# Ranking's row sums moved from VectorE to ScalarE over four row buffers, and the projection's bias moved from GpSimd to VectorE

## The reference, cut to what matters

```python
score = einsum('bc,bnc->bn', gt, kproj) * SCALE         # per batch, after a layer norm of x
probs = softmax(score, axis=-1)
order = argsort(-probs, axis=-1)                        # 3136 tokens ranked
reserve = order[:, :1568]
...                                                     # merging, attention with top-k, back to tokens
out = (full + x_prune) @ W_proj + b_proj                # then x + out, layer norm, routing to 8 experts
```

## Time and profile before

| what | us |
|---|---|
| median of 3 runs | 11960.32 (11940.51 to 11967.36) |
| the profiled execution | 11958.84 |
| its span | 11957.0 |
| `rank` with the constants, about 0 to 1411 | 1411 |
| `merge`, about 1411 to 3010 | 1599 |
| `attend`, about 3010 to 10368 | 7358 |
| `project`, about 10368 to 11089 | 721 |
| `experts`, about 11089 to 11957 | 868 |

### The profile page before, as it was taken

One profiled execution on the slowest core, in us unless ns is written; L12 is line 12 of the kernel. 1 busy time (PEld: TensorE's weight loads), 2 busy tenths in 40 slices (PEclk: granted clock), 3 DMA queues, 4 the chain that ended last, 5 costly groups with the idle time before them and its releaser, 6 DMA issues. The chain is left out here.

```text
span 11957.0 us, 167569 instructions
## 1 busy us (share of the span) xinstructions
PE 8171.2 (68%) x45521; PEld 5352.0 (45%) x45521; DVE 9191.7 (77%) x26006; ACT 6947.3 (58%) x11527; POOL 2151.1 (18%) x1960
## 2 busy tenths in 40 slices
PE   5555477777486765667878687876667768343899
PEld 4555455555243433334444344443334434233787
DVE  8999644444898988999999899998889989644333
ACT  0000011221697976878999799997788979122222
POOL 2323211111000000000000000000000000277666
PEclk9999955555566655656666666665666656555555
DMA  3222100000000000000000000000000000243211
GB/s 91 73 68 72 33 19 20 20 19 21 14 16 16 17 12 14 13 16 17 17 17 18 14 15 18 18 18 14 13 14 17 18 12 16 43 96 79 55 54 40
DMA packets 669893, 352.03 MB, mean 29 GB/s; under 512 B 587281, under 2 KB 605680, under 8 KB 665056
## 3 DMA queue, kind: packets, MB, share of 16 engines
q1 hardware_dynamic: 607920, 242.84, 9.5%
q0 software_dynamic: 58624, 60.72, 2.0%
q10 hardware_dynamic: 2384, 37.11, 0.9%
HBM read 200.20 MB, written 147.72 MB: 29 GB/s over the span
## 5 line engine op out<-in xcount | busy, mean ns | idle before, releaser
L1049 PE MATMUL a_psT<-a_qt,a_kt 74*122 74x366 bf16 x3456 | 1554.8, 450 | 969.1 <-ACT a_pT L1130 632.0
L1138 ACT ACTIVATE a_junk<-a_s,a_aim 122x1097 bf16<-122x1097 f32 x1152 | 1378.9, 1208 | 721.3 <-DVE a_s L1281 721.3
L1214 DVE MAX8 a_near<-a_below 122x8 f32<-122x274 f32 (+1 forms) x4608 | 1699.2, 430 | 0.1
L1052 PEld LDWEIGHTS a_psT<-a_weigh,a_drops 122*122 122x122 bf16 x10368 | 1571.0, 190 | 192.0
L1207 DVE SCALAR_TENSOR_TENSOR a_below<-a_s,a_te,a_signs 122x1097 f32<-122x1097 f32 x1152 | 1546.4, 1352 | 129.2 <-remote 128.3
L1130 ACT ACTIVATE a_pT<-a_psT 122x732 f32<-122x732 f32 (+1 forms) x1920 | 1371.6, 715 | 455.4 <-PE a_psT L1052 447.9
L1052 PE MATMUL a_psT<-a_weigh,a_drops 122*122 122x122 bf16 x10368 | 1522.5, 273 | 0.0
L1138 ACT ACTIVATE a_signs<-a_s,a_te 122x1097 bf16<-122x1097 f32 x1152 | 1400.9, 1219 | 4.4 <-DVE a_te L1199 4.4
L1065 PE MATMUL a_psO<-a_pT,a_v 122*32 122x366 f32 x6912 | 1401.3, 698 | 0.0
L1138 ACT ACTIVATE a_junk<-a_s,a_te 122x1097 bf16<-122x1097 f32 x1152 | 1389.2, 1209 | 0.0
L1049 PEld LDWEIGHTS a_psT<-a_qt,a_kt 74*122 74x122 bf16 x3456 | 616.8, 178 | 1667.0 <-issue 1648.1
(11 more groups left out here) (356 smaller groups left out, 14795.9 us busy)
## 6 DMA issues: line engine op xcount, KB each, us to landing
xbuf<-r_blank ACTq DMA_DIRECT2D x16, 1990.6 KB
e_xg<-xbuf SPq DMA_DIRECT2D x56, 568.8 KB, 4.3
r_bc<-pr SPq DMA_DIRECT2D x16, 1372.0 KB, 7.4
a_k<-kT SPq DMA_DIRECT2D x384, 51.5 KB
a_q<-qT SPq DMA_DIRECT2D x384, 51.5 KB
a_kt<-kT SPq DMA_DIRECT2D x384, 51.5 KB
a_qt<-qT SPq DMA_DIRECT2D x384, 51.5 KB
r_xt<-in_x SPq DMA_DIRECT2D x16, 784.0 KB
```

Of the source, the lines that this page charges most:

```text
L1049: pe.matmul(out[:, x, 0:CW], kt[q][:, u * QP:(u + 1) * QP], qt[q][:, c * CW:(c + 1) * CW], start=True, stop=False)
L1052: mm = pe.matmul(out[:, x, t * QP:(t + 1) * QP], drops[:, c * CT + t, u * QP:(u + 1) * QP], weigh[:, :], start=False, stop=t == CT - 1)
L1138: act.activation(out[:, :], s_[:, t, :], ACT.Sign, bias=at[:, t:t + 1], scale=-1.0, accum_out=total[:, t:t + 1]).then_inc(counted[r], 1)
L1214: mx = dve.max(near[:, t, g, :], below[t % 3][:, EDGES[g]:EDGES[g + 1]])
```

## The change

In `rank` the comparison no longer adds up its rows (except for the last tile). ScalarE reads the marks of tile j and copies them to a scratch buffer with an accumulating output, which gives the row sums. VectorE waits for this count (`row_counted`) beside TensorE's before it writes over a mark buffer, and once more at a batch's end. ScalarE's square and root for the next batch come behind its copies 1 and 6. The parts are placed behind other comparisons. The rows `xls` and the indices get four buffers instead of two, and the body of a batch is written out twelve times (four, a loop that turns twice over four, four).

In `project` the bias is added by VectorE: batches 0 and 1 ahead of everything, batch b + 2 behind `seat(b)`. GpSimd issues no tensor instruction there any more. `merge` clears 17 semaphores of the ranking before its first load.

```diff
-BEHIND = [0, 1, 8, 10, 11, 12, 13, 14, 15, 16]
+BEHIND = [0, 5, 10, 12, 13, 14, 15, 16, 17, 18]
+LAPS = 4
...
-        xls = [sb(f"r_xl{u}", [TP, NT, C + 1]) for u in range(2)]
+        xls = [sb(f"r_xl{u}", [TP, NT, C + 1]) for u in range(LAPS)]
...
+        spill = [sb(f"r_spill{i}", [TP, N], BF16) for i in range(2)]
...
+            for u in range(LAPS):
+                body(0, u, True, True)
+            if B > 2 * LAPS:
+                with eng.Fori(1, B // LAPS - 1) as i:
+                    for u in range(LAPS):
                         body(i, u, False, True)
+            for u in range(LAPS):
+                body(B // LAPS - 1, u, False, u < LAPS - 1)
...
         @block.scalar
-            with act.Fori(0, B) as b:
+            def body(i, u, first, more):
+                b = LAPS * i + u
                 act.dma_start(d.xbuf[...], blank[...]).then_inc(cleared, 16)
+                for j in range(NT - 1):
+                    act.wait_ge(compared, (NT - 1) * b + j + 1)
+                    if j >= 2 or not first or u:
+                        act.wait_ge(row_counted, (NT - 1) * b + j - 1)
+                    act.activation(spill[(u + j) % 2][:, j * TP:N], greater[j % MARKS][:, j * TP:N], ACT.Copy,
+                                   accum_out=cnt[:, 1, j:j + 1]).then_inc(row_counted, 1)
+                    if more and j == BEHIND[0] + 1:
+                        square(b + 1)
+                    if more and j == BEHIND[1] + 1:
+                        deviate(b + 1)
...
         @block.vector
                     if j >= MARKS:
                         dve.wait_ge(added, (NT - 1) * b + j - MARKS + 1)
-                    more_ = dve.tensor_scalar(greater[j % MARKS][:, at:N], bc[:, at:N], rk[:, j:j + 1], None, ALU.is_gt,
-                                              ALU.add, accum_out=cnt[:, 1, j:j + 1])
+                        dve.wait_ge(row_counted, (NT - 1) * b + j - MARKS + 1)
                     if j < NT - 1:
-                        more_.then_inc(compared, 1)
+                        dve.tensor_scalar(greater[j % MARKS][:, at:N], bc[:, at:N], rk[:, j:j + 1], None,
+                                          ALU.is_gt).then_inc(compared, 1)
...
-                            dve.wait_ge(scattered[1 - u], 16 * NT * (i + u))
+                        v = (u + 1) % LAPS
+                            dve.wait_ge(scattered[v], 16 * NT * (i if v else i + 1))
...
+                dve.wait_ge(row_counted, (NT - 1) * (b + 1))
...
 merge, sync:
+            for used in k.used:
+                sp.sem_clear(used)
             rows(0)
...
 project, gpsimd:
-            def bias(b):
-                pool.wait_ge(x_in[u], 16 * (b // 2 + 1))
-                pool.tensor_tensor(xts[u][:, :, :], xts[u][:, :, :], bproj[...].to_broadcast([TP, NT, C]),
-                                   ALU.add).then_inc(biased, 1)
-            bias(0)
-            bias(1)
             place(pool, k, d, B - 1, 0, srcs, dsts, src_in, dst_in, put)
             for b in range(B):
-                if b + 2 < B:
-                    bias(b + 2)
 project, vector:
+            def bias(b):
+                dve.wait_ge(x_in[b % 2], 16 * (b // 2 + 1))
+                dve.tensor_tensor(xt[:, :, :], xt[:, :, :], bproj[...].to_broadcast([TP, NT, C]),
+                                  ALU.add).then_inc(biased, 1)
+            bias(0)
+            bias(1)
             normalise(0)
             for b in range(B):
                 if b + 1 < B:
                     normalise(b + 1)
                 choose(b)
                 seat(b)
+                if b + 2 < B:
+                    bias(b + 2)
```

More of the change, by code:

```diff
@@ L219, in rank @@
         rks = [sb(f"r_rk{u}", [TP, NT]) for u in range(2)]
-        idxs = [sb(f"r_idx{u}", [TP, NT], U32) for u in range(2)]
+        idxs = [sb(f"r_idx{u}", [TP, NT], U32) for u in range(LAPS)]
         minus = sb("r_minus", [TP, 1], BF16)
@@ L267, in body @@
                 row = d.pr[bass.ds(b * NT, NT), :].rearrange("(a j) p -> a (j p)", a=1)
-                sp.dma_start(bcs[u][:, :], row.partition_broadcast(TP)).then_inc(prob_in, 16)
+                sp.dma_start(bcs[u % 2][:, :], row.partition_broadcast(TP)).then_inc(prob_in, 16)
                 sp.dma_start(d.y[bass.ds(b * N, N), :].rearrange("(j p) c -> p j c", p=TP), xls[u][:, :, 0:C]).then_inc(laid[u], 16)
             batches(sp, body)
-            for u in range(2):
-                sp.wait_ge(laid[u], 16 * (B // 2))
+            for u in range(LAPS):
+                sp.wait_ge(laid[u], 16 * (B // LAPS))
         @block.scalar
@@ L340, in body @@
                     if more and j in BEHIND[2:2 + len(parts)]:
-                        parts[BEHIND.index(j) - 2](b + 1, 1 - u)
+                        parts[BEHIND.index(j) - 2](b + 1, (u + 1) % LAPS)
             pe.wait_ge(started, 2)
@@ L364, in _ @@
             batches(pool, body)
-            for u in range(2):
-                pool.wait_ge(scattered[u], 16 * NT * (B // 2))
+            for u in range(LAPS):
+                pool.wait_ge(scattered[u], 16 * NT * (B // LAPS))
         @block.vector
@@ L435, in probabilities @@
                 link.then(dve.reciprocal(col[0:TP, 5:6], pc[0:TP, 3:4]))
-                dve.tensor_scalar(rks[u][:, :], e, col[0:TP, 5:6], None, ALU.mult).then_inc(probbed, 1)
+                dve.tensor_scalar(rks[u % 2][:, :], e, col[0:TP, 5:6], None, ALU.mult).then_inc(probbed, 1)
             def as_rows(b, u):
@@ L444, in body @@
             def body(i, u, first, more):
[L445 to L446 removed]
+                b = LAPS * i + u
+                bc, rk, idx = bcs[u % 2], rks[u % 2], idxs[u]
                 dve.wait_ge(prob_in, 16 * b + 16)
@@ L462, in body @@
                     if more and j in BEHIND:
-                        if j == BEHIND[2] and not (first and u == 0):
-                            dve.wait_ge(scattered[1 - u], 16 * NT * (i + u))
-                            dve.wait_ge(laid[1 - u], 16 * (i + u))
-                        parts[BEHIND.index(j)](b + 1, 1 - u)
+                        v = (u + 1) % LAPS
+                        if j == BEHIND[2] and not (first and v):
+                            dve.wait_ge(scattered[v], 16 * NT * (i if v else i + 1))
+                            dve.wait_ge(laid[v], 16 * (i if v else i + 1))
+                        parts[BEHIND.index(j)](b + 1, v)
                 link.all()
```

38 lines of the change are left out of this document (18 added, 20 removed).

## The result

The kernel after takes 11626.08 us (median of 4 runs, 11608.52 to 11637.99), the one before 11950.42 (4 runs): ratio 0.9734, 95% interval 0.9717 to 0.9750. The direction came as forecast, and so did what gains and what waits; the ranking's gain was put too small. The profiled execution after took 11615.7 us (span 11614.0, before 11957.0).

What follows compares the result with a forecast made beforehand. VectorE was taken to bound the ranking, GpSimd the projection. Ranking -254, projection -30, rest +2 sum to -282 us; from the profiled 11958.8 that gives 11677, with the runs' median 1.5 higher 11678; range 11635 to 11785.

Steps and rivals of the forecast that it cites:

- the lock: Ranking: fast VectorE instructions and GpSimd's scatters wait for each other at shared ports; 0.5 us per batch for VectorE.
- the rival of 1.047: Ranking: ScalarE becomes the bound at 1.047 ns per column or more loads, a batch of 72, total 11740; chance 0.10.
- Two table loads of 1.28: Ranking, ScalarE: two table loads of 1.28 us per batch, counted in its total of about 50 us.
- Where the queues meet: Ranking: VectorE's waits for other engines after the change, together 9.3 us, making a batch of 67.0.
- the ring of mark buffers: Ranking: VectorE's waits for ScalarE to free one of four mark buffers, put at 3.5 us per batch.
- the walk: Ranking: one batch's queues laid side by side; mark-buffer waits of 0.6, 0.9, 0.8 at comparisons 8, 9, 10, together 2.3 us.
- Four row buffers: Ranking: removes the scatter wait, 3.6 us in about every second batch, and leaves two loop turns of six, 3.3 each.
- GpSimd beside VectorE: Ranking: scatters and fast VectorE instructions delay each other; VectorE loses 0.5 us, a batch of 67.5; GpSimd keeps up.
- one comparison in half of them: Ranking: half of GpSimd's scatters wait for at most one VectorE comparison, 0.3 to 1.9 us.
- a double wait for all: Ranking: each scatter waits for two comparisons, GpSimd becomes the bound at 74 us per batch, total 11759; chance 0.15.
- the slower kernel: Ranking: VectorE's fast comparisons starve GpSimd's scatters, a batch of 98 us, total 12174; chance 0.03.
- third rival: Ranking: ScalarE becomes the bound, a batch of 72 us, sum given as -190, total 11740; chance 0.10.

Runs made afterwards that it cites:

- e5: Kernel after with a one-column exponential on ScalarE ahead of every square, to bring back two table loads per batch: 11634.67 us, ratio 0.9736.
- e3: Kernel after with two row buffers and two index buffers instead of four, laps of two bodies: 11907.13 us, ratio 0.9953.
- e1: Kernel after with the projection's bias put back on GpSimd: 11668.48 us, ratio 0.9755.
- e4: Kernel after with the old comparison, VectorE summing the rows and ScalarE copying nothing, four row buffers kept: 11886.73 us, ratio 0.9939.
- e2: Kernel before with only the projection's bias moved to VectorE: 11923.84 us, ratio 0.9970.

## Why the prediction was right or wrong

- **What bounds the kernel: right.** The ranking gained with VectorE's queue, the projection with GpSimd's; merge did not move.
- **Comparison: right.** 29.6 us per batch for 29.4. The first batch, with no scatters beside it, has 29.3: in the comparisons the lock costs VectorE 0.3 us of a batch. Over all its instructions a batch takes 54.4 us of busy time for the first one's 53.7, in the kernel before 77.2 for 77.0. So the whole lock costs about the 0.5 that I took, up to 0.7.
- **ScalarE's copies: right for the copies, wrong for the two table loads.** 0.839 ns a column for 0.833, so the rival of 1.047 is dead; 43 us of a batch for the 45.4. "Two table loads of 1.28" were carried over from the kernel before without asking whether the new loop still has them; it has none.
- **Where the queues meet: the step that failed.** The term that was mis-sized is the wait for the ring of mark buffers: "I put the ring at 3.5, above the 2.3 of this walk, since each new wait also has its signal's way". The runs show 0.6 us of a batch. e5, which has the walk's two loads, waits 1.9, where the walk had 2.3, and at the walk's three comparisons. So of the 2.9 us too many about 1.2 are the loads that the new loop doesn't have, 1.2 the signals' way, which no trace shows, and 0.4 the walk itself. Over 15 batches that is 43 us, against the 48 by which the ranking gained more than forecast. The rest of the 2.6 us between the predicted pitch of 67.5 and 64.9 is small and of both signs: the last counts 0.4 for 1, the lock 0.5 to 0.7 for 0.5, the row of probabilities 1.7 for 1, sums 3.6 for 3.4, gate 1.8 for 1.9. The mean before was 84.2 over 14 batches, 0.3 below the 84.5 that I set against it.
- **Four row buffers: right in what they remove, poor in what they are for.** The scatter wait is gone. I priced the buffers by the wait of the kernel before (3.6 in every second batch) and did not ask what the faster comparison would make of it: 20 us in every batch (e3). The one loop turn that the trace after shows as a wait took 5.6 us, where one took 3.3 before.
- **GpSimd beside VectorE: right in kind.** A scatter takes 1504 ns for 974; by my "one comparison in half of them" it would have been about 0.55 longer. A single scatter waits through two comparisons at times, though, so the bound of one was wrong. The rivals of a double wait for all, and of the slower kernel, did not come. "The last scatter ends later by what GpSimd carries over: +5" did come, at 3.2 us; the sign that a batch's last scatter is out before the next batch's begin holds for all but the last batch.
- **The ranking's sum:** -254 predicted, -301.7 measured: 15 batches -291.7 for -255, the last batch -13.1 for -8 up to its indices, GpSimd's carry-over +3.2 for +5, and nothing of the +4 for code.
- **Projection: right in kind, small in size.** -35.5 for -30. A batch is 38.6 for 39.2, since the scatter beside the bias loses 1.04 us (1.97 for 0.93) and the pitch 0.8, not 1.4. The start cost 1.4.
- **Rest.** The clears: 1.1 for 2. "Attention and experts are untouched" holds for their code and not for their time: +10.3 and -17.9 in the profiled execution, the experts' by the granted clock; e1 to e4, whose attention takes from 7354.3 to 7379.1 us for the 7366.5 of after and 7356.2 of before, show nothing that ties either to the change.
- **The range.** Faster was given 0.95. The lower end, 11635, is said to be "a batch of 65, projection at its best", but the prediction's own terms don't add up to it: from the 11960.3 on which 11678 stands, 15 x 19.5 = 292.5 and 8 less, 9 more, 48 less and 2 more make 11623. Added up rightly the range would have held the measured 11626, but by luck, with a projection at -48 that came to -35.5. (The third rival's sum is off too: 15 x 12.5 less 4 is 183.5, not 190.) And its batch of 65 was not the bound of 63 that the walk's section had given; the batch came to 64.9.

## What to carry to other kernels

Where an edit makes one queue faster, price every buffer and every wait by what the neighbours will do then, not by its wait in the profile of before: the comparison alone was worth 6.5 us, the buffers alone 40, both together 301. When a wait is taken per batch, leave out a batch of another kind: here the last one alone held 6.6 of the ring's 16.2 us. When two engines wait for each other in turns, lay both queues side by side, trust the walk, and look at what else each queue owes there; moving a part to cover a wait only helps if the engine that is waited for isn't busy with the work that stands in the gap. Judge such edits by the pitch of the stage and not by the total, whose other stages scatter by more than the edit is worth.

## What the runs showed of the hardware

- Beside plain f32-to-bf16 comparisons of VectorE an indirect DMA of GpSimd gets longer. Of the 448 in the ranking after, 247 saw no comparison end and took 0.93 to 0.95 us. 54 ended 0.8 us and 13 ended 1.1 us behind the comparison in which they had started; 131 ended 0.1 us behind one that had begun while they ran, the longest after 3.56 us. The mean is 1.50 us for 0.97. VectorE's comparisons take 29.6 us of a batch beside the scatters and 29.3 without.
- A table load of ScalarE took its 1.28 us and no more. In e5 the load ahead of the exponential starts at 594.68, 0.02 us behind the copy's accumulator read, and the exponential at 595.97; the load ahead of the root starts at 609.91 and the root at 611.20. The two together raised VectorE's ring wait by 1.2 us a batch. The Trainium skill (ScalarE: Activation LUTs, "What ACT_TABLE_LOAD costs") adds a drain and gives about 2.66 us for a switch; here no drain of that length shows, and the measurement decides.
- Squares, roots and accumulating copies need no load between them: in the trace after there is one load ahead of the first square and one ahead of the first root, and none with the 15 others of each and the 432 copies. The kernel before, with square and root alone in a loop, has 32.
- TensorE's granted clock rose from 1.2 to 2.4 GHz for 37 us in the middle of a stage in which it had been busy without a pause for the 100 us before, in some of the profiled executions (after, e1, e3) and not in others (before, e2, e4). The eleven chunks of the experts from 11159.5 to 11304.5 took 145.0 us there, against 15.2 each at 1.2 GHz: 22 us.
